# Second attention rebuilt: one projection for queries and keys, three stacked parts and one score product per tile

## What is computed

```python
qk = layernorm(x)                      # (8, 128, 512), cut into 4 patches of 128 columns
q = Wq @ qp + bq ; k = Wk @ qp + bk    # (64, 128) per patch, from the same rows
val = Wv @ ctx_patch + bv              # (64, 128)
scores = q_h.T @ k_h / sqrt(8)         # 8 heads of 8 rows each
scores = where(mask > 0, scores, -1e9)
o = softmax(scores) @ v_h ; o = gelu(o)
x = x + tanh(g) * (Wo @ o + bo) * mask
```

## Time and profile before

| | us |
|---|---|
| median of 3 runs | 1082.39 (1081.38 to 1086.38) |
| the profiled execution | 1082.77 |
| its span on the core | 1080.9 |
| TensorE busy | 959.7 (89%) |
| VectorE busy | 619.8 (57%) |
| GpSimd busy | 424.6 (39%) |
| ScalarE busy | 337.3 (31%) |

### The profile page before, as it was taken

One profiled execution on the slowest core, in us unless ns is written; L12 is line 12 of the kernel. 1 busy time (PEld: TensorE's weight loads), 2 busy tenths in 40 slices (PEclk: granted clock), 3 DMA queues, 4 the chain that ended last, 5 costly groups with the idle time before them and its releaser, 6 DMA issues.

```text
span 1080.9 us, 14248 instructions
## 1 busy us (share of the span) xinstructions
PE 959.7 (89%) x4851; PEld 737.6 (68%) x4851; DVE 619.8 (57%) x1067; ACT 337.3 (31%) x599; POOL 424.6 (39%) x414
## 2 busy tenths in 40 slices
PE   4899999999998999999999979979999998629991
PEld 4677778877777777778777658637777674227770
DVE  5864764465752665653647655645655555873334
ACT  4322142132241141331221311225444556312320
POOL 3541522421620522422415243464333424764540
PEclk9899999999999999999999998979999995659996
DMA  8020110010200110200200211060000003213447
GB/s 288 10 79 1 68 40 10 36 43 30 78 1 12 40 39 30 78 1 10 78 1 1 70 44 54 17 226 21 11 10 10 0 1 114 92 56 124 147 127 262
DMA packets 37592, 63.77 MB, mean 59 GB/s; under 512 B 5601, under 2 KB 13217, under 8 KB 37409
## 3 DMA queue, kind: packets, MB, share of 16 engines
q1 hardware_dynamic: 32416, 50.70, 13.7%
q0 software_dynamic: 3680, 12.06, 3.4%
q10 hardware_dynamic: 1440, 0.24, 0.1%
HBM read 52.77 MB, written 10.22 MB: 58 GB/s over the span
## 4 chain that ended last, share of the span: by engine, by line
PE 81%; DVE 8%; issue 4%; DMA 2%; ACT 2%; POOL 2%; ACTq 1%; SPq 0%; POOLq 0%; DVEq 0%
PE ps L1289 17%; PE ps L1290 16%; PE ps L1291 16%; PE ps L1501 5%; PE ps L1378 5%; PE ps L1520 5%; PE ps L1386 4%; PE ps L1508 3%; PE ps L1394 2%; PE ps L1488 2%; DVE at_lo L969 1%; DMA rows_in<-h_rows,gather_i 1%; DVE stats L844 1%; PE ps L1528 1%; POOL k_blk L543 1%
## 5 line engine op out<-in xcount | busy, mean ns | idle before, releaser
L476 POOL TENSOR_TENSOR q_t<-rot_a,rot_b 128x512 f32<-128x512 f32 x64 | 82.3, 1287 | 145.8 <-DVE rot_b L894 145.8
L1289 PE MATMUL ps<-wo_hi,at_hi 128*128 128x512 f32 x256 | 108.7, 425 | 18.7 <-DVE at_lo L969 11.9
L892 DVE TENSOR_TENSOR rot_a<-ps,cos 128x512 f32<-128x512 f32 x80 | 55.3, 692 | 112.6 <-PE ps L1291 112.6
L543 POOL TENSOR_TENSOR k_blk<-k_raw,m_full 32x512 f32<-32x512 f32 x64 | 80.8, 1262 | 90.1 <-ACT k_raw L752 86.3
L1289 PE MATMUL ps<-xt_hi,wq_hi 128*128 128x512 f32 x256 | 108.1, 422 | 0.2 <-issue 0.2
L1291 PE MATMUL ps<-xt_hi,wq_lo 128*128 128x512 f32 x256 | 101.4, 396 | 0.0
L1290 PE MATMUL ps<-xt_lo,wq_hi 128*128 128x512 f32 x256 | 101.4, 396 | 0.0
L1291 PE MATMUL ps<-wo_hi,at_lo 128*128 128x512 f32 x256 | 100.2, 391 | 0.0
L1290 PE MATMUL ps<-wo_lo,at_hi 128*128 128x512 f32 x256 | 100.0, 391 | 0.0
L697 ACT ACTIVATE at_hi<-ps 128x512 fp32r<-128x512 f32 x64 | 38.2, 597 | 189.2 <-PE ps L1394 189.2
L974 DVE TENSOR_TENSOR X<-ps,X 128x512 f32<-128x512 f32 x64 | 44.3, 691 | 84.6 <-PE ps L1291 84.6
(11 more groups left out here) (219 smaller groups left out, 2206.3 us busy)
## 6 DMA issues: line engine op xcount, KB each, us to landing
wq_raw<-in_wq SPq DMA_DIRECT2D x8, 1024.0 KB, 5.6
wo_raw<-in_wo SPq DMA_DIRECT2D x8, 1024.0 KB, 5.3
w_raw<-in_we SPq DMA_DIRECT2D x8, 1024.0 KB, 9.6
y_in<-y_rows SPq DMA_DIRECT2D x16, 256.0 KB, 5.1
X<-in_x SPq DMA_DIRECT2D x4, 512.0 KB, 13.3
wk_raw<-in_wk SPq DMA_DIRECT2D x8, 256.0 KB, 2.8
q_t<-in_ctx_t SPq DMA_DIRECT2D x2, 1024.0 KB, 10.4
wv_raw<-in_wv SPq DMA_DIRECT2D x4, 512.0 KB, 4.5
```

The source lines that it names most:

```text
L476: nc.gpsimd.tensor_tensor(dst, rot_a[:, r % 2, :], rot_b[:, r % 2, :], ALU.add).then_inc(rope_ok, 1)
L543: last = nc.gpsimd.tensor_tensor(k_blk[part, j, grp, :, hd, :], heads(k_raw[part, grp, :]), heads(m_full[part, j, :]), ALU.mult)
L892: nc.vector.tensor_tensor(heads(rot_a[:, r % 2, :]), heads(bank), bcast(cos[:, :], 4), ALU.mult)
L1289: nc.tensor.matmul(dst, w_hi, x_hi, start=start and k == 0, stop=False)
```

## The change

- One projection per batch: wqk1 holds Wq and Wk side by side (64 + 64 columns), so one f32 product of h gives queries in rows 0 to 63 and keys in rows 64 to 127.
- VectorE moves it out of PSUM (`evict`): bias added and, on the key rows, times the mask, `keep` (1 on query rows). ScalarE rounds it to fp32r (`round_qk`), GpSimd takes the remainder (`remainder`).
- SP copies parts of 32 rows inside SBUF (`stack`): for each of two head groups k3 = (high, low, high) and q3 = (high, high, low), 96 rows; row 96 of q3 is ones, and row 96 of k_blk is the mask penalty `pen`, copied by DMA as well. Per batch 12 copies of parts and 2 of the penalty.
- GpSimd spreads k3 over k_blk: one product of 96 rows per tile, with `diag` choosing the head. k_blk needs no memset any more.
- A score tile is one fp32r product over 97 rows.
- Rows, projection and eviction run two batches ahead. Those of batches 0 and 1 move into the mixing stage, with p_w and PSUM bank 7 as their places.
- The loops of the two stages are written out instead of Fori. An expert load follows each context load on SP. Constants of the old padding are gone. In the last layer some semaphores are merged; what is computed there is the same.

```diff
             def stack(b):
+                sp.wait_ge(qkl_ok, CREDIT + b + 1)
+                if b >= 1:
+                    sp.wait_ge(kb_ok, CREDIT + H1 * b)
+                for g in range(2):
+                    rows = slice(E1 + g * half, E1 + (g + 1) * half)
+                    for n, part in enumerate((qk_hi, qk_lo, qk_hi)):
+                        sp.dma_start(k3[n * half:(n + 1) * half, g, :].bitcast(F32), part[rows, :].bitcast(F32)).then_inc(k3_in[g], 16)
+                if b == 0:
+                    sp.wait_ge(pen_ok, CREDIT + 3)
+                if b >= 2:
+                    sp.wait_ge(s2_mm, CREDIT + H1 * (b - 1))
+                for g in range(2):
+                    rows = slice(g * half, (g + 1) * half)
+                    for n, part in enumerate((qk_hi, qk_hi, qk_lo)):
+                        sp.dma_start(q3[n * half:(n + 1) * half, j, g, :].bitcast(F32), part[rows, :].bitcast(F32)).then_inc(q3_in[j], 16)
+                    sp.dma_start(k_blk[PARTS:PARTS + 1, j, g, :, :, :].bitcast(F32),
+                                 pen[b:b + 1, :, :, :]).then_inc(pen_in[j], 16)
+            stack(0)
+            stack(1)
             sp.wait_ge(x2_ok, CREDIT + B)
-            for e in range(FIRST):
-                load_expert(e)
             for b in range(2, B):
-                sp.wait_ge(pq_mm, CREDIT + 5 * (b - 1))
+                stack(b)
+                sp.wait_ge(vc_mm, CREDIT + b - 1)
                 load_ctx(b, b % 2)
+                if b - 2 < FIRST:
+                    load_expert(b - 2)
...
+            def keys(b):                                        # GpSimd
+                for u in range(H1):
+                    patch, g = divmod(u, 2)
+                    if u < 2:
+                        gp.wait_ge(k3_in[g], 48 * b + 48)
+                    if b >= 2:
+                        gp.wait_ge(s2_mm, CREDIT + H1 * (b - 2) + u + 1)
+                    nc.gpsimd.tensor_tensor(k_blk[0:PARTS, b % 2, g, patch, :, :], bcast(k3[0:PARTS, g, patch * P:(patch + 1) * P].bitcast(F32), HG),
+                                            diag[0:PARTS, 0:HG].unsqueeze(2).to_broadcast([PARTS, HG, P]), ALU.mult).then_inc(kb_ok, 1)
+            gp.wait_ge(late_in, 16 * N_LATE)
+            remainder(1)
+            for b in range(B):
+                keys(b)
+                if b + 2 < B:
+                    remainder(b + 2)
...
+            def round_qk(b):                                    # ScalarE, at u == 3 of batch b - 2
+                ac.wait_ge(qk_ev, CREDIT + b + 1)
+                if b >= 1:
+                    for g in range(2):
+                        ac.wait_ge(k3_in[g], 48 * b)
+                    ac.wait_ge(q3_in[1 - b % 2], 48 * (b + b % 2))
+                hi_part(qk_hi[:, :], qk_raw[:, :], qkh_ok)
...
+            def evict(b, j, bank=0):                            # VectorE, at u == 3 of batch b - 2
+                ve.wait_ge(qk_mm, CREDIT + b + 1)
+                ve.wait_ge(qkl_ok, CREDIT + b)
+                ve.wait_ge(keep_ok, CREDIT + b + 1)
+                nc.vector.scalar_tensor_tensor(qk_raw[:, :], ps[:, bank, :], bqk[:, 0:1], keep[:, j, :], ALU.add, ALU.mult).then_inc(qk_ev, 1)
+            mix(1, 1)
+            nc.vector.memset(q3[PARTS:PARTS + 1, :, :, :].bitcast(F32), 1.0).then_inc(pen_ok, 1)
+            ve.wait_ge(pen_raw, 16)
+            nc.vector.tensor_scalar(mask_8[:, :], mask_8[:, :], 0.0, MASKED, ALU.is_gt, ALU.mult).then_inc(pen_ok, 1)
+            ve.wait_ge(pen_ok, CREDIT + 2)
+            nc.vector.tensor_scalar(pen[:, :, :, :], mask_8[:, :].rearrange("b (a k) -> b a k", a=PATCH).unsqueeze(2).to_broadcast([B, PATCH, HG, P]),
+                                    -MASKED, None, ALU.add).then_inc(pen_ok, 1)
+            for b in range(2, B):
+                mix(b, b % 2, last=b == B - 1)
+                row_stats(2, b - 2, b % 2, x2_ok)
+                if b == B - 3:
+                    ve.wait_ge(maskb_in, 16 * B)
+                    rows(0, 0, p_w)
+                    kept(0, 0)
+                if b == B - 2:
+                    evict(0, 0, 7)
+                    rows(1, 1, p_w)
+                    kept(1, 1)
+            evict(1, 1, 7)
...
             def scores(b, j, u):                                # TensorE
+                pe.wait_ge(kb_ok, CREDIT + H1 * b + u + 1)
+                if u == 0:
+                    pe.wait_ge(q3_in[j], 48 * (b - j) + 96)
+                    pe.wait_ge(pen_in[j], 16 * (b - j) + 32)
                 pe.wait_ge(sb_ok, CREDIT + 8 * b + u - 1)
-                nc.tensor.matmul(ps[:, 2 + u % 2, :], q_pad[:, j, u % 2, (u // 2) * P:(u // 2 + 1) * P],
-                                 k_blk[:, j, u % 2, u // 2, :, :], start=True, stop=True).then_inc(s2_mm, 1)
+                nc.tensor.matmul(ps[:, 2 + u % 2, :], q3[0:PARTS + 1, j, u % 2, (u // 2) * P:(u // 2 + 1) * P],
+                                 k_blk[0:PARTS + 1, j, u % 2, u // 2, :, :], start=True, stop=True).then_inc(s2_mm, 1)
...
-                    if not last and 1 <= u <= 5:
-                        proj(b + 1, 1 - j, u - 1)
+                    if more and u == 1:
+                        pe.wait_ge(qk_ev, CREDIT + b + 2)
+                        proj(b + 2, j, h, 0)
+                    if not last and u == 3:
+                        context(b + 1, 1 - j)
```

More of the change, by code:

```diff
@@ L773, in batch @@
                         out_turned(b - 1, 1 - j)
-                    if not last and 2 <= u <= 5:
-                        proj_out(b + 1, 1 - j, u - 2)
-            for n in range(4):
-                proj_out(0, 0, n)
+                    if more and u == 3:
+                        round_qk(b + 2)
             batch(0, 0, first=True)
-            with ac.Fori(0, (B - 2) // 2) as i:
-                batch(2 * i + 1, 1)
-                batch(2 * i + 2, 0)
-            batch(B - 1, 1, last=True)
+            for b in range(1, B):
+                batch(b, b % 2, more=b + 2 < B)
             turned(B - 1, H1 - 1)
@@ L1118, in _ @@
             batch(0, 0, first=True)
-            with ve.Fori(0, (B - 2) // 2) as i:
-                batch(2 * i + 1, 1)
-                batch(2 * i + 2, 0)
-            batch(B - 1, 1, last=True)
+            for b in range(1, B):
+                batch(b, b % 2, more=b + 2 < B, last=b == B - 1)
             over_sums(B - 1, 1)
@@ L1465, in mix, with proj @@
                     lora_out(b - 1, 1 - j)
+            def proj(b, j, rows, bank):
+                pe.wait_ge(hc_ok, CREDIT + b + 1)
+                nc.tensor.matmul(ps[:, bank, :], wqk1[:, :], rows[:, j, :], start=True, stop=True).then_inc(qk_mm, 1)
             turn_rows(1, 0, 0, 0)
             mix(0, 0, first=True)
[L1469 to L1472 removed]
+            for b in range(1, B):
+                mix(b, b % 2, last=b == B - 1)
+                if b >= B - 2:
+                    pe.wait_ge(qk_ev, CREDIT + b - B + 2)
+                    proj(b - B + 2, b % 2, p_w, 7)
@@ L1530, in turn_out, with batch @@
                 last.then_inc(ot_mm, 1)
-            def batch(b, j, first=False, last=False):
+            def batch(b, j, first=False, more=True, last=False):
                 for u in range(H1):
@@ L1550, in batch @@
                         turn_out(b - 1, 1 - j)
-            for n in range(5):
-                proj(0, 0, n)
+            context(0, 0)
             scores(0, 0, 0)
@@ L1556, in _ @@
             batch(0, 0, first=True)
-            with pe.Fori(0, (B - 2) // 2) as i:
-                batch(2 * i + 1, 1)
-                batch(2 * i + 2, 0)
-            batch(B - 1, 1, last=True)
+            for b in range(1, B):
+                batch(b, b % 2, more=b + 2 < B, last=b == B - 1)
             turn(B - 1, H1 - 1)
```

267 lines of the change are left out of this document (113 added, 154 removed).

## The result

| | before | after |
|---|---|---|
| median of 4 runs, us | 1082.32 (1081.38 to 1086.38) | 1124.78 (1116.51 to 1125.08) |
| the profiled execution, its span | 1082.77, 1080.9 | 1124.47, 1122.6 |
| granted clock over the span | 0.942 | 0.855 |
| end of the second attention, us | 899.5 | 941.2 |

The account below looks back on a forecast made before the run. TensorE, mostly at the low clock, was taken to bound the second attention: 712.0 + 194.1 (eight batches of 24.8, less 4.3) + 2.2 = 908.3 against 899.5, so 1082.8 us becomes about 1091; 8 in 10 range 1048 to 1126.

Parts of the forecast that it names:

- Slower, by the clock: Second attention: thin TensorE work keeps the clock low for most of it; chance of a slower kernel 0.55.
- the forecast itself: Second attention: a third of TensorE's work at the high clock; 1091 us, range 1072 to 1110, chance 0.48.
- TensorE's prices: TensorE in the second attention: a batch takes 15.3 us at the full clock, 29.5 at the low one.
- The share of the high level: Second attention: a third of TensorE's work runs at the full clock, making 24.8 us a batch.
- the sum: Second attention: start 712.0, batches 194.1 after taking off 4.3, end waits 2.2; end at 908.3 us.
- the ring: Second attention: GpSimd's keys, SP's copies, ScalarE's rounding and GpSimd's remainder wait in turn, 19.4 us a batch (18.3 to 20.6).
- the second rival: Second attention: clock low throughout, 29.5 us a batch, 1128 us; chance 0.20.
- The context load at nothing: SP in the second attention: the context load behind the copies is issued early enough to cost nothing.
- The first rival: Second attention: the clock holds and the ring binds at 19.4 us a batch, 1050 us; chance 0.25.
- The start: Entry of the second attention: first score product at 712.0 us against 707.1 today; no gain, no loss.
- a sign of being wrong by the prediction: Second attention: TensorE waiting for k_blk or q3 at a low clock, or clock 1.00 until 895, would refute it.

Follow-up runs that it names:

- the filler: Useless f32 products (identity times X) put ahead of score products; with 512 columns ahead of all 64 in the changed kernel, 1098.96 us.
- two buffers: Changed kernel with two buffers each for qk_hi and qk_lo, so rounding and remainder don't wait for the previous batch's copies: 1114.87 us, ratio 1.0299.
- 64 columns of filler: Kernel with both pauses removed, VectorE's work spread and a filled start, plus 64 useless columns ahead of each later score product: 1054.28 us (1040.01 to 1097.31).
- the last experiment: Changed kernel with context load ahead, double qk_hi and qk_lo, 128 useless columns per score product, but VectorE's order unchanged and no start products: 1137.09 us.
- the spread and the start: o_n, eviction, rounding and remainder moved apart; thirteen useless products before, 512 columns ahead of, the first five scores; with both pauses removed, 1077.52 us.
- the first burst: Changed kernel with nine useless f32 products of 512 columns between batch 0's context product and its first score product: 1120.78 us (1116.03 to 1129.22).

## Why the prediction was right and where it was wrong

**Slower, by the clock: right.** The measured median lies near the upper end of the 8 in 10 range, 1048 to 1126, and above the 1072 to 1110 of the forecast itself. The direction rested on the stretch from 890 to 894 us of the kernel before, where full records of turns and sums lost the clock. The 120 us at 0.50 with 118.76 us busy are that reading, thirty times as long; the filler, which makes the kernel faster by adding work, shows the cause and not only the coincidence.

**TensorE's prices: right.** A low batch was put at 29.5 us and measures 29.34; a tile at 3.05 and measures 2.98, high at 1.57 and measures 1.57.

**The share of the high level: the step that failed.** "I take a third of TensorE's work at the high level" had no row under it. From the first score product at 713.7 to the end at 941.2 the stage took 227.4 us, where the sum had 196.3. With the same corrections (4.3 less, 2.2 more) that is 28.7 us a batch, and between 15.3 and 29.5 a share of 0.06, pauses included. Two errors stand in it. The clock was at 1.00 for 23.9 of the 227.4 us, and without its waits TensorE took 212.5 us, which by the prediction's own prices is a sixth of the work at the high level and not a third, some 18 us. And TensorE stood still for 14.9 us where the sum had 2.2: 4.3 for the ring, 5.9 for the context, the rest for VectorE and the first keys. These 31 us and 1.7 of the start are the 33 us between 1091 and the profiled 1124.5. The forecast had a projection or o_n bring the clock back, until the next pause. That happened: the clock rose at 722.6, 865.9, 879.6 and 930.8, each time within 4 us of the start of one of them. But the projections at 744, 775, 804 and 833 brought nothing, nor did five of the seven turns of o_n before the last, and the high stretches lasted 3 to 10 us. The case whose number came nearest is the second rival, low throughout: 1128 against 1124.8, to which I gave 0.20. That it is so near is partly luck: it has neither the high stretches, worth 18 us, nor the 13 us of waits, and the two nearly cancel. For it I had the right sentence ("nothing as dense as the 5.2 us is left") and didn't weigh it.

**The ring: right in kind, two terms off.** It was put at 19.4 us and measures 20.3: SP issues a copy of 32 rows in 0.59 us, 0.63 apart, outside my bounds of 0.32 and 0.51, and the eight key products take 8.36 us, not 10.55. The first took DMAs between memory and SBUF for copies inside SBUF, the second a product of 32 rows of another form. From batch 2 on it is hidden: GpSimd waits up to 19.9 us for the rounding. At the first boundary it did what was described, exponentials behind the rounding, and cost the first high stretch.

**The context load at nothing: wrong.** "Issued with over 10 us to go before the next stack" looked at the stack and not at the product that needs the load. Behind the fourteen copies the load of batch 7 landed 4.7 us after TensorE asked for it, and 9.0 us late once the ring was gone. At the low clock the wait for it was 1.2 us, at the end of a high stretch 4.7 us.

**The first rival, the ring at full clock, had 1050.** With the ring and the context load mended and the clock kept by filler it is 1040. The time was there to be had; the change as made did not reach it, and with both mended, the tile spread and no filler the clock was still lost for 100 us in a row.

**The start: right.** First score product 713.7 (712.0), the gain nil; two buffers move it to 710.8, where the penalty rows bind. The one wait for k_blk at a low clock behind it, a sign of being wrong by the prediction, is 0.20 us for the second key product of batch 0.

The Trainium skill, page "TensorE: Matmul & The Clock Gate", section "HAM oscillation — how this bites in real kernels", describes a kernel in which every wait for a DMA brings the low clock back, and the cure is to reorder the loop so that TensorE stays busy. The waits for ctx_s here agree (4.9 us, then 11 us at 0.50). The fall at 810 us with 64 columns of filler, and the 100 us at 0.50 with full records, are not of that kind: there was no wait to avoid.

What stays open: why the same tile keeps the clock at one time and loses it at another without a wait, and why a tile with 64 useless columns stayed at 1040 to 1045 us in three of six runs and took 1063 to 1097 in the others; and which of the products that were taken out would be enough to keep it. In the last experiment the spread and the start were taken away together; its traced execution had the clock at 1.00 from 718.4 to 756.0, so there the start is not what lost it, but no run takes the spread away alone.

## What to carry to other kernels

Before taking wide products out of a loop, look at what is left between turns and narrow products, and price the loop at both levels of the clock; a stage whose TensorE is the bound can lose more by the clock than it gains by the work removed (here 8 us a batch less at the full clock by the sum, 6 more at the low one as measured). If the loop is still worth it, remove first every place where TensorE runs dry, short ones too, and then try a small product without use in each tile: measured in the kernel as a whole, since 128 columns with short gaps left made it slower still, and 512 with all pauses left gave back only 26 of 42 us. And a load that stood at no one's heels before must be followed to its consumer when fourteen others are put ahead of it.

## What the hardware showed that was not expected

- Useless work makes this kernel faster: 128 columns per tile, some 14 us of TensorE time in the stage, are worth 37 us against the same kernel without them (medians 1040.0 and 1077.5), and the spread shrinks from 35 to 7 us.
- The same stream without a gap held either level in one execution of one kernel: twice 22 us at 1.00 and 100 us at 0.50. Between them a high stretch of 3.4 us was lost with TensorE busy throughout.
- A gap of 0.75 to 0.76 us at the high level of the changed tile was followed by the low level in all 18 cases, the nine above and nine in the traces of the change, the first burst and the two buffers; in three of these a longer wait had begun before the fall.
- A gap of 0.54 us was followed by 26 us at 0.50, while gaps of 0.54 and 0.83 us in the same kernel, 10 to 19 us earlier, left the clock at 1.00.
- A copy of 32 rows inside SBUF costs SP 0.59 us per issue and lands after 2.0 us.
- GpSimd's product of 96 rows by 512 with two broadcast operands takes 1.05 us, less than the 1.26 us of the kernel before's over 32 rows.
